# A fused attention and expert kernel: mask rows by transfer, one product moved into the scores, and equal weight rows copied

## The reference

```python
def _L0_xattn_ref(hidden_states, memory_tokens, memory_mask):
    scores = einsum('bsd,bmd->bsm', hidden_states, memory_tokens) * scale
    scores = where(memory_mask[:, None, :], scores, -1e30)
    attn = softmax(scores, axis=-1)
    readout = einsum('bsm,bmd->bsd', attn, memory_tokens)
    return where(any(memory_mask)[:, None, None], readout, 0)

def _L0_ffn_ref(x, G, gate_w, up_w, down_w, lora_A, lora_B):   # 8 experts, 2 per token
    scores = softmax(x @ G); w = the two largest, at their experts
    gated = silu(x @ gate_w) * (x @ up_w)                       # 64 wide per expert
    out = einsum('bsef,bse,ehf->bsh', gated, w, down_w)
    return out + einsum('bser,bse,ehr->bsh', x @ lora_A, w, lora_B)

x = x + _L0_xattn_ref(_layernorm(x), ctx, mask)
x = x + _L0_ffn_ref(_layernorm(x), ...)
```

## Time and profile before

| | |
|---|---|
| median of 3 runs | 531.66 us (531.63 to 532.07) |
| profiled execution | 531.73 us |
| span in its trace | 529.9 us |
| mean granted TensorE clock | 0.989 |
| busy: PE, PEld, DVE, ACT, POOL | 501.9, 438.4, 471.1, 345.5, 286.8 us |
| moved by DMA | 189.12 MB, mean 357 GB/s |
| end of the sweep, start of the passes | about 211 us |

### The profile page before, as it was taken

One profiled execution on the slowest core, in us unless ns is written; L12 is line 12 of the kernel. 1 busy time (PEld: TensorE's weight loads), 2 busy tenths in 40 slices (PEclk: granted clock), 3 DMA queues, 4 the chain that ended last, 5 costly groups with the idle time before them and its releaser, 6 DMA issues.

```text
span 529.9 us, 16395 instructions
## 1 busy us (share of the span) xinstructions
PE 501.9 (95%) x4040; PEld 438.4 (83%) x4040; DVE 471.1 (89%) x1921; ACT 345.5 (65%) x927; POOL 286.8 (54%) x397
## 2 busy tenths in 40 slices
PE   8999999999999999688899999999999999999894
PEld 7887888888888777577788899888999999999782
DVE  5999999999999987578898999998899999999785
ACT  4787888777887787466677778787444444444331
POOL 4337776777777677544443444444444454444434
PEclk9999999999999999899999999999999999999988
DMA  8899999999999989999997999958999999999722
GB/s 327 316 404 331 409 408 390 399 392 392 406 389 402 374 288 317 381 376 372 353 319 290 368 405 368 351 227 315 416 414 415 417 414 416 417 413 414 307 81 81
DMA packets 65609, 189.12 MB, mean 357 GB/s; under 512 B 9582, under 2 KB 9710, under 8 KB 65520
## 3 DMA queue, kind: packets, MB, share of 16 engines
q1 hardware_dynamic: 44352, 120.20, 60.7%
q0 software_dynamic: 20800, 67.65, 32.1%
q10 hardware_dynamic: 368, 0.22, 0.2%
HBM read 114.04 MB, written 78.73 MB: 364 GB/s over the span
## 4 chain that ended last, share of the span: by engine, by line
PE 75%; issue 10%; DVE 6%; ACT 6%; another core or an unknown queue 1%; POOL 1%; POOLq 0%; ACTq 0%; DVEq 0%
PE bank L515 13%; PE rd L515 12%; PE bank L493 11%; PE rd L531 7%; PE bank L366 6%; PE rd L532 6%; PE rd L406 4%; PE rd L522 3%; PE bank L345 3%; PE rd L407 3%; PE rd L379 3%; ACT xn L601 2%; ACT prob L621 1%; PE rd L454 1%; PE rd L386 1%
## 5 line engine op out<-in xcount | busy, mean ns | idle before, releaser
L670 ACT COPY hT<-bank 128x512 f32<-128x512 f32 x140 | 81.9, 585 | 54.8 <-PE bank L493 50.6
L515 PE MATMUL bank<-wg_sb,hT 128*128 x560 | 81.5, 289 | 0.4 <-issue 0.4
L515 PE MATMUL rd<-wg_sb,hT 128*128 x560 | 81.2, 289 | 0.0
L366 PE MATMUL bank<-cc_sb,xnT 128*128 128x136 f32 x512 | 80.1, 286 | 0.0
L1237 POOL DMA_INDIRECT x_rows<-xe x64 | 65.3, 1020 | 23.2 <-issue 19.5
L515 PEld LDWEIGHTS bank<-wg_sb,hT 128*128 128x128 f32 x560 | 73.5, 192 | 0.9 <-issue 0.9
L515 PEld LDWEIGHTS rd<-wg_sb,hT 128*128 128x128 f32 x560 | 73.6, 192 | 0.1
L531 PE MATMUL rd<-dn_a,ggT_a 128*128 x140 | 67.5, 482 | 4.9 <-issue 3.2
L366 PEld LDWEIGHTS bank<-cc_sb,xnT 128*128 128x128 f32 x512 | 68.3, 191 | 1.1
L1252 POOL DMA_INDIRECT out_x<-z_shared x41 | 40.0, 975 | 42.6 <-issue 36.0
L1127 DVE SCALAR_TENSOR_TENSOR z_shared<-rd,z_shared 128x512 f32<-128x512 f32 x77 | 57.7, 749 | 1.9
(11 more groups left out here) (167 smaller groups left out, 1202.3 us busy)
## 6 DMA issues: line engine op xcount, KB each, us to landing
cc_sb<-in_cc SPq DMA_DIRECT2D x64, 532.0 KB
z_shared<-z_rows SPq DMA_DIRECT2D x41, 516.0 KB
x_sb<-in_x SPq DMA_DIRECT2D x64, 256.0 KB
z_own<-z_rows SPq DMA_DIRECT2D x29, 516.0 KB
z_shared<-x_rows SPq DMA_DIRECT2D x36, 260.0 KB
z_own<-x_rows SPq DMA_DIRECT2D x34, 260.0 KB
z_rows<-pad SPq DMA_DIRECT2D x8, 516.0 KB
wg_sb<-in_wg SPq DMA_DIRECT2D x8, 288.0 KB
```

Source lines behind the costliest of these rows:

```text
L366: mm = pe.matmul(sc_ps[:, 0:S + E], xnT[:, n % 2, k, :], by_feature(n, k, S + E), start=False, stop=(k == KD - 1))
L515: mm = pe.matmul(gu_ps[q % 2][:, 0:GU], hT[:, q % 2, k, :], wg_flat[:, bass.ds(at + k * GU, GU)], start=(k == 0), stop=(k == KD - 1))
L670: act.copy(hT[:, q % 2, :, :], hT_ps[q % 2][:].rearrange("p (k s) -> p k s", k=KD)).then_inc(hT_ready, 1)
```

## The change

Four things are changed.

1. From tile 16 on, TensorE no longer adds the bias row. SyncE writes `bias` to memory once (`mask_rows`) and brings eight tiles' rows at a time back to all 128 partitions in six transfers (`SPREAD_AT` gives their place in its queue). They lie in buffers that the passes use later (two slots of z_own, and hT). VectorE's masking takes that bf16 row in place of `zeros`.
2. `context_by_g` stands in the middle of the scores, behind `turn_prob`, and no longer behind the scores.
3. The odd pieces of the down weights load only their last 32 rows. ScalarE makes the rounded part of those rows alone, and copies the first 96 rows from the finished piece before (`down_same`), for which it waits for POOL. POOL clears `dn_hi[:, 1, :]` once. ScalarE's weight steps stand ahead of `keep_xT`; the second of them is a tick later than before.
4. SyncE waits for `pad` just ahead of the first transfer that needs it.

```diff
+MR = 8
+SPREAD_AT = {2: 12, 3: 20, 4: 27, 5: 36, 6: 44, 7: 51}
...
+        def spread(i):
+
+            rows = hT[:].rearrange("p j k s -> p (j k s)") if i >= 6 else z_own[:, (i - 2) // 2, :]
+            at = i % 2 * (MR * S // 2)
+            return rows[:, at:at + MR * S // 2].bitcast(BF16)
+
...
+        def down_rows(i):
+
+            return slice(0, P) if i % 2 == 0 else slice(KG, P)
...
-            sp.wait_ge(pad_set, 2)
             for n in range(5, B):
+                if n == 7:
+                    sp.wait_ge(bias_ready, 2)
+                    sp.dma_start(mask_rows[:], bias[0:B, 0:S]).then_inc(mask_kept, 16)
+                for i in [i for i, at in SPREAD_AT.items() if at == n]:
+                    sp.wait_ge(mask_kept, 16)
+                    sp.dma_start(spread(i), bass.AP(tensor=mask_rows.tensor, offset=i * MR * S, ap=[[0, P], [1, MR * S]])).then_inc(mask_spread[i], 16)
...
+                    if n == 10:
+                        sp.wait_ge(pad_set, 2)
                     sp.dma_start(x1_rows[at:at + P, :], pad[:, D:ZW]).then_inc(padded[0], 16)
...
-                    sp.dma_start(dn_part(i).bitcast(F32), dn[:, i % 2, i // 2, :]).then_inc(dn_loaded, 16)
+                    if i % 2 == 0:
+                        sp.dma_start(dn_part(i).bitcast(F32), dn[:, i // 2, :]).then_inc(dn_loaded, 16)
+                    else:
+                        sp.dma_start(dn_part(i)[KG:P, :].bitcast(F32), dn_rest[:, i // 2, :]).then_inc(dn_loaded, 16)
...
             scattered(BA)
+            sp.wait_ge(masked_ready, 6 * MR)
...
-                pe.matmul(sc_ps[:, 0:S + E], tile_of[:, n:n + 1].broadcast_to([P, S]), bias[:], start=True, stop=False)
+                if n < 2 * MR:
+                    pe.matmul(sc_ps[:, 0:S + E], tile_of[:, n:n + 1].broadcast_to([P, S]), bias[:], start=True, stop=False)
                 for k in range(KD):
                     if k == KD // 2 and n >= 1:
                         turn_prob(n - 1)
-                    mm = pe.matmul(sc_ps[:, 0:S + E], xnT[:, n % 2, k, :], by_feature(n, k, S + E), start=False, stop=(k == KD - 1))
+                        if n % 2 == 1:
+                            context_by_g(n // 2)
+                    mm = pe.matmul(sc_ps[:, 0:S + E], xnT[:, n % 2, k, :], by_feature(n, k, S + E), start=(n >= 2 * MR and k == 0), stop=(k == KD - 1))
...
-                if in_sweep(t, 2) and t % 2 == 0:
-                    context_by_g((t - 2) // 2)
...
-                act.activation(dn_hi[:, i % 2, :].bitcast(F32R), dn_part(i).bitcast(F32), ACT.Copy, scale=const_sb[:, SIGN:SIGN + 1]).then_inc(dn_hi_ready, 1)
+                if i == 1:
+                    act.wait_ge(dn_hi_set, 1)
+                own = down_rows(i)
+                act.activation(dn_hi[own, i % 2, :].bitcast(F32R), dn_part(i)[own, :].bitcast(F32), ACT.Copy, scale=const_sb[own, SIGN:SIGN + 1]).then_inc(dn_hi_ready, 1)
+
+            def down_same(i):
+
+                act.wait_ge(dn_ready, i)
+                act.copy(dn_part(i)[0:KG, :], dn_part(i - 1)[0:KG, :].bitcast(F32)).then_inc(dn_low_left, 1)
...
+                if t + 2 in SUMS_AT:
+                    down_hi(SUMS_AT.index(t + 2))
+                if t in SUMS_AT:
+                    i = SUMS_AT.index(t)
+                    if i % 2 == 0:
+                        down_left(i)
+                    else:
+                        down_same(i)
                 if in_sweep(t, 0):
                     keep_xT(t)
...
-                if t + 2 in SUMS_AT:
-                    down_hi(SUMS_AT.index(t + 2))
-                if t + 1 in SUMS_AT:
-                    down_left(SUMS_AT.index(t + 1))
...
-                dve.tensor_tensor_reduce(masked[:, n % 2, :], sc_ps[:, 0:S], zeros[:], -SCALE, 3e38, ALU.add, ALU.min,
+                i, b = divmod(n, MR)
+                if i >= 2 and b == 0:
+                    dve.wait_ge(mask_spread[i], 16)
+                hidden = zeros[:] if i < 2 else spread(i)[:, b * S:(b + 1) * S]
+                dve.tensor_tensor_reduce(masked[:, n % 2, :], sc_ps[:, 0:S], hidden, -SCALE, 3e38, ALU.add, ALU.min,
                                          rowmin[:, n % 2, :]).then_inc(masked_ready, 1)
...
                 pool.wait_ge(dn_low_left, i + 1)
+                pool.wait_ge(dn_hi_ready, i + 1)
...
+            pool.memset(dn_hi[:, 1, :], 0.0).then_inc(dn_hi_set, 1)
```

More of the change, by code:

```diff
@@ L93, with xattn_moe @@
 NCONST = PACK + len(GROUPS)
-def xattn_moe(nc, x, cc, mask, wg, dn, g, consts, out):
+def xattn_moe(nc, x, cc, mask, wg, dn, dn_rest, g, consts, out):
     with ExitStack() as stack:
@@ L179, in rows_of @@
             return z_own[:, slot, :] if slot < RO else z_shared[:, slot - RO, :]
+        mask_rows = nc.dram_tensor("mask_rows", (B, S), BF16).ap()
         x1_rows = nc.dram_tensor("x1_rows", (ROWS, XW), F32).ap()
@@ L188, in xattn_moe @@
             sem, ("const_loaded", "g_loaded", "wg_loaded", "dn_loaded", "dn_hi_ready", "dn_low_left", "dn_ready"))
-        mask_loaded = sem("mask_loaded")
+        mask_loaded, mask_kept = sem("mask_loaded"), sem("mask_kept")
+        mask_spread = {i: sem(f"mask_spread{i}") for i in SPREAD_AT}
         set_up, ones_set, pad_set, before_ready = sem("set_up"), sem("ones_set"), sem("pad_set"), sem("before_ready")
@@ L200, in xattn_moe @@
             sem, ("strips_done", "strips_ready", "prod_done", "prod_ready", "part_ready"))
-        after_set = sem("after_set")
+        after_set, dn_hi_set = sem("after_set"), sem("dn_hi_set")
         top_ready, which_ready, pair_ready, gap_step, turn_step, lexp_ready, hot_ready = map(
@@ L1305 @@
     down, lora_b = down.transpose(2, 0, 1), lora_b.transpose(2, 0, 1)
-    back = np.stack([np.concatenate([down[:Q], lora_b, lora_b, down[Q:], again], 0) for again in (down[:Q], down[Q:])], 1)
+    back = np.concatenate([down[:Q], lora_b, lora_b, down[Q:], down[:Q]], 0)
     consts = np.zeros((P, NCONST), np.float32)
@@ L1326 @@
         consts[j * GP:j * GP + E, at:at + E] = np.eye(E)
-    arrays = {"x": x, "cc": cc, "mask": mask, "wg": into, "dn": back, "g": g, "consts": consts}
+    arrays = {"x": x, "cc": cc, "mask": mask, "wg": into, "dn": back, "dn_rest": down[Q:], "g": g, "consts": consts}
     arrays = {f"in_{n}": np.ascontiguousarray(a) for n, a in arrays.items()}
```

## The result

The changed kernel takes 541.07 us (median; 540.02 to 541.28), the kernel before 531.87 us on the same chip: ratio 1.0156, 95% interval 1.0108 to 1.0204. I had forecast 531.2 us, range 528.7 to 533.2. The change makes the kernel slower by some 9 us, outside the range and on the side to which I gave 0.20.

What follows compares the result with a forecast made beforehand. VectorE was taken to pace the sweep, TensorE with ScalarE its last ticks, TensorE the passes. Span 529.9 - 2.3 (steady) + 1.9 (end) = 529.5, plus 1.8 around it: 531.3, stated as 531.2 us; range 528.7 to 533.2.

Steps and rivals of the forecast that it cites:

- the steady term: Sweep from about tile 16 to 56: earlier readout and scores fill VectorE's idle time, -2.3 us, bounds -3.6 and -0.5.
- on even ticks this closes within about 0.1 us of TensorE's own path: Sweep: scores waiting in their middle for ScalarE's strips copy give back only 0 to 0.25 us per cycle.
- sum of 0.29: Scores per four tiles: earlier by 0.35 (readout) and 0.07 (bias), later by 0.13 (context product), 0.29 us net.
- Mask transfers: Sweep: six transfers of 256 KB, bytes balanced by smaller weight loads and covered by slots five ticks ahead, 0 us.
- crowding: Rival (4): mask transfers crowd the loads and TensorE waits for contexts, up to +4.0 us, 532 to 535; chance 0.06.
- uncovered bound of 4.0 us: Sweep: cost of the six mask transfers if uncovered, at 0.66 us of DMA time each.
- The end, +1.9: Last ticks: the weight copies at tiles 59 and 63 wait for POOL, making the sweep's end 1.9 us later.
- recovery to +0.9: Tiles 60 to 62: the lateness of +1.7 us at tile 59 shrinks to +0.9 at tile 62.
- bound without recovery: End of the sweep: upper bound of +3.3 us, the two waits' 1.7 and 1.6 with nothing regained between.
- Start and pads, 0: Start: SyncE's 4.1 us wait for `pad` goes, but neither TensorE nor VectorE waited for a transfer there, 0 us.
- Rival (2): Start of passes: the end's 1.9 us vanish in the 4.61 us wait, the gain shows whole, 529.4 us; chance 0.33.
- Rival (3): Sweep: the strips' loop limits the gain to 0.5 us, the end costs 1.9 to 2.5, 533.1 to 533.7; chance 0.19.

Runs made afterwards that it cites:

- context_alone: Kernel before with only the context product moved amid the scores: 535.82 against 528.07 us, ratio 1.0141.
- context_again: Kernel before with only the context product amid the scores, once more on another chip: 521.11 against 513.58 us, ratio 1.0136.
- weights_whole: Kernel before with the weights' part of the change, but parts 13 and 15 loaded whole and worked out by `down_left`: 509.71 us, ratio 0.995.
- whole_again: weights_whole once more, with more rounds, on another chip: 509.96 us, ratio 0.9925 to the kernel before.
- whole_no_rows: whole_mask without its mask transfers, so the mask is left out from tile 16 on: 510.66 us, ratio 0.9934 to the kernel before.
- whole_early: weights_whole with the context product amid the scores and the strips' copy ahead of the normalisation of x: 511.05 us, ratio 0.995 to the kernel before.
- mask_alone: Kernel before with only the mask's part (six transfers, no bias matmul from tile 16, VectorE reads the rows): ratio 1.006.
- weights_alone: Kernel before with only the weights' part (odd parts' first rows copied, ScalarE's weight steps moved): ratio 1.0013.
- strips_early: Changed kernel with ScalarE's copy of the strips ahead of the normalisation of the next x tile: ratio 1.0172 to the kernel before.
- context_back: Changed kernel with the context product moved back behind the scores: ratio 1.0158 to the kernel before.
- after_again: The changed kernel, unaltered, once more on another chip: 521.63 against 513.67 us, ratio 1.0134.
- before_again: The kernel before, unaltered, one execution for its trace on the chip of after_again, where that kernel takes 513.67 us.
- whole_mask: weights_whole with the mask's part of the change added, transfers ahead of the loads: 514.19 us, ratio 1.0003 to the kernel before.
- whole_mask_behind: whole_mask with each mask transfer issued behind its tick's loads of context and x: 513.12 us, ratio 0.9977 to the kernel before.
- pads_alone: Kernel before with only the wait for the pad moved to the pad's first use: ratio 1.0033.

## Why the prediction was wrong

**The size of the steady term, -2.3 us: it came as +4.6.** The step that failed is "on even ticks this closes within about 0.1 us of TensorE's own path, so some of it comes back, 0 to 0.25 us per cycle". I priced the copy by its length (0.27) and took for granted that it starts when its inputs are there. On the first chip it started 0.5 to 1.0 us later in one pair of two, and TensorE stood there. With the weight step still ahead of the copy (context_alone, context_again) the loss is 1.4% on both chips tried. The other half of the term was right: with the weight steps moved the mean cycle goes from 12.5 to 12.13 us (weights_whole) and 12.20 (whole_again), where I had reckoned 0.35 us for the readout that no longer waits. That the sum of 0.29 comes near too is in part luck, since these kernels have neither the 0.07 of the bias matmul nor the 0.13 of the product in them, and neither showed: whole_no_rows gained nothing, whole_early lost nothing.

What delays the copy is open. The lag stands in the first traces of the changed kernel and of the kernel before and, on a second chip, in those of mask_alone and weights_alone, so neither the place of the product nor the bias matmul makes it; on the chips measured later, strips_early, context_back, after_again and context_again have none. In after_again tile 58 is only 1.7 us further behind than tile 3, VectorE waits 0.3 us for the scores, and its waits for x are 3.4 us against 2.1 in before_again. Yet the whole is nearly as slow: in its trace 6.7 us are lost up to tile 63, and 4.4 more in the passes.

**Mask transfers: "I take 0".** This term failed, though not on the first chip: there VectorE doesn't wait for x from 20 to 180 us in the changed kernel's trace either. I read that no engine waited for a transfer and that the slots lie five ticks ahead, and gave crowding 0.06. The row against it was in the prediction: a DMA share of 1.03. On another chip the same kernel before did wait, 2.1 us (before_again). The uncovered bound of 4.0 us was close to what was measured: 3.1 and 3.2 us (whole_mask against whole_early, whole_mask_behind against whole_again). That VectorE and not TensorE waits I had not foreseen. The bias matmuls that go gave nothing, which fits VectorE as the bound. That the bytes balance against the smaller weight loads over the whole sweep did not keep the change from waiting for x (after_again, 3.4 us).

**The end, +1.9: right mechanism, too small.** The masking of tile 59 was forecast 1.7 us late, and came 5.67 us behind tile 58 in place of 3.95: 1.7. The recovery to +0.9 by tile 62 did not come (tiles 59 to 62 take 9.2 us before and 9.4 after), and the second wait added 1.1. The sum is 2.9, near my bound without recovery, 3.3. weights_whole confirms the cause by its absence: tiles 58 to 63 take 15.4 us in place of 20.25 in weights_alone.

**Start and pads, 0.** In the first chip's trace 3.2 us were lost, probably most of them by the clock: whole_mask_behind, at the low clock, is at tile 3 at 23.38 us, whole_mask at 20.05. after_again loses 1.7 at full clock, with 5.6 us of waits for x up to 20 us against 4.4 in before_again. The pad's later wait is not shown to be the cause: pads_alone lost nothing there, and whole_mask_behind, without it, has the low clock in its trace as well. Among 18 traces it is in these two. What tips it is open.

**Rival (2)** rested on the unnamed wait of 4.61 us at the start of the passes. About 1.6 us of what the sweep lost did vanish there. But the wait does not come with the kernel alone: before_again starts its passes without it.
```profile
215.22 0.22 ACT L676 ACTIVATE th<-bank 128x64 f32<-128x64 f32 x1 [0.30 <-PE bank L515]
```
This kernel queues the same pads, so they don't make the wait by themselves. On the first chip the first tanh starts 13.1 us after SyncE begins to queue them (206.91) in the kernel before, and 15.1 us after (214.47) in the changed one, so nothing shows that it ended with them. What makes it is open. Whether the rule of the Trainium skill (Runtime: NRT & Kernel Launch, Instruction fetch mechanics), that an engine refills its instructions through a DMA queue of its own, has a part in it, no run here shows.

**Rival (3)**, the strips' loop, named the right place and side, 533.1 to 533.7 us; it took the loop for as long as its parts, and so was short by the copy's lag and the transfers. In after_again the passes too took 4.4 us longer than in before_again, in a profiled execution 2.6 us over its median (524.19 against 521.63); that is not explained. The price of the bf16 row (289 ns) was right, and in the sweep that of the wait for the pad.

## What to carry to other kernels

When a step is moved into the middle of a critical group, its input must be ready with slack: look at what stands in the queue ahead of the producer, and move that first. With the strips' copy ahead of xn the same move cost nothing.
A DMA share that is full (1.03 here) leaves no room even if no engine waits yet: here 1.5 MB more cost 3.1 to 3.2 us of the 4.0 that they take to move, whatever engine they relieve.
Take a change of four parts apart: one of them (the weights' part, without the two late copies) held the whole gain, 0.5 to 0.75%, 0.3% by the place of its steps alone, hidden beneath the losses of the others.

## What the runs showed of the hardware that I had not expected

- Chips differ by more than the change: the kernel before takes 513.2 to 513.7 us on three of them, 528.07 and 531.87 on two. The sweep is alike (masking of tile 63 at 209.25 us in the first trace, 208.83 in before_again); it is the passes that differ, 309.9 against 296.4 us from the first tanh to the end.
- A weight step on 32 partitions takes 716 ns, one on 128 takes 718: fewer partitions saved ScalarE nothing.
- TensorE's clock can fall to the lower level for 6.8 us near the start, in an execution whose engine had stood 1.00 us ahead of its first scores. It fell after a stand of 0.74 us too (whole_mask_behind), and stayed full after one of 1.25 (context_alone); the same code ran on another chip at full clock (after_again).
